# Moving one tile's normalise-and-Gelu step ahead of the other tile's statistics in a two-tile feed-forward block

## The reference

```python
x = _layernorm(x + attn(x))        # softmax over the query axis, causal mask
x = _layernorm(x + ffn(x))
def ffn(x):                        # three blocks
    h = x
    for blk in range(3):
        i0, i1 = (2 * blk, 2 * blk + 1)
        y = _qlora_linear(h, qweights[i0], ...)     # 1024 x 1024, dequantised, plus a rank-32 part
        y = _layernorm(y, ln_gamma[blk], ln_beta[blk])
        y = jax.nn.gelu(y, approximate=False)
        y = _qlora_linear(y, qweights[i1], ...)
        h = y + h
    return h
```

## Time and profile before

| | |
|---|---|
| median of 8 runs | 2744.24 us |
| the profiled execution | 2743.9 us |
| its span, slowest core (of 2724.1 to 2742.3) | 2742.3 us |
| TensorE busy with matmuls | 1659.6 us, 61% |
| VectorE busy | 1034.7 us, 38% |
| ScalarE busy | 1035.7 us, 38% |
| GpSimd busy | 130.3 us, 5% |
| mean granted clock of TensorE, slowest core | 0.795 |

### The profile page before, as it was taken

The page is one execution under the profiler, slowest core; times in us unless marked ns, Lnnn a source line. Parts: engine busy times, 40 slices in busy tenths (PEclk is TensorE's granted clock), DMA queues, the critical chain, the costliest instruction groups (busy, mean ns, idle before and its releaser), DMA issues.

```text
span 2742.3 us, 21892 instructions; the slowest of 8 cores (2724.1 to 2742.3 us)
## 1 busy us (share of the span) xinstructions
PE 1659.6 (61%) x6880; PEld 690.0 (25%) x6880; DVE 1034.7 (38%) x1001; ACT 1035.7 (38%) x1517; POOL 130.3 (5%) x112
## 2 busy tenths in 40 slices
PE   0999891396989111115658555776467656665853
PEld 0444330143433000002223222332123222222321
DVE  2113435301343734442532733255414526152262
ACT  0421113242111213324454445445454454545444
POOL 0000003300000500000000000000000000000000
PEclk9999995698999555557879758988678787687985
DMA  6200134501012086774100050110230000511001
GB/s 198 90 30 16 46 108 154 183 16 54 16 46 77 23 278 233 243 246 164 62 31 31 0 184 31 47 46 0 76 139 31 31 31 1 184 33 60 31 1 62
DMA packets 72542, 228.62 MB, mean 83 GB/s; under 512 B 6768, under 2 KB 7024, under 8 KB 66032
## 3 DMA queue, kind: packets, MB, share of 16 engines
q1 hardware_dynamic: 61680, 181.09, 20.0%
q0 software_dynamic: 10752, 46.14, 4.3%
HBM read 181.07 MB, written 46.14 MB: 83 GB/s over the span
## 4 chain that ended last, share of the span: by engine, by line
PE 48%; ACT 16%; DVE 13%; DMA 11%; issue 8%; PEld 2%; DVEq 1%; PEldq 1%; SPq 0%; ACTq 0%; POOL 0%; POOLq 0%
PE ps L857 23%; PE ps L298 8%; PE ps L420 5%; DMA weffs<-PL 4%; PE ps L361 4%; ACT PL L1033 3%; PE ps L837 2%; PEld ps L496 2%; PE ps L1085 2%; DVE PL L1025 2%; DVE PL L1023 2%; DMA PL<-xt 2%; DVE PL L627 2%; DVE PL L624 2%; PE ps L839 2%
## 5 line engine op out<-in xcount | busy, mean ns | idle before, releaser
L857 PE MATMUL ps<-PL 128*128 128x512 bf16 x3072 | 737.6, 397 | 249.2 <-ACT PL L1033 237.6
L857 PEld LDWEIGHTS ps<-PL 128*128 128x128 bf16 x3072 | 309.9, 101 | 655.7 <-issue 328.6
L298 PE MATMUL ps<-PL 128*128 128x512 bf16 x1024 | 229.9, 388 | 170.1 <-DVE PL L214 65.3
L1001 DVE TENSOR_TENSOR e2s<-e2s,m2s 128x512 f32<-128x512 f32 x32 | 22.1, 691 | 555.5 <-ACT e2s L993 555.5
L725 PE MATMUL ps<-PL 32*128 32x512 bf16 x48 | 28.1, 586 | 301.9 <-DVEq L748 205.3
L880 ACT ACTIVATE PL<-ps,fb 128x512 bf16<-128x512 f32 x192 | 131.9, 687 | 162.6 <-PE ps L839 162.3
L893 DVE SCALAR_TENSOR_TENSOR PL<-ps,fb,PL 128x512 f32<-128x512 f32 x192 | 144.2, 751 | 88.6 <-PE ps L857 88.1
L298 PEld LDWEIGHTS ps<-PL 128*128 128x128 bf16 x1024 | 101.6, 100 | 298.0 <-issue 183.2
L1085 PE MATMUL ps<-eye,PL 128*128 128x128 f32 x256 | 87.2, 436 | 142.8 <-ACT PL L1099 77.9
L496 PE MATMUL ps<-PL 128*128 128x512 bf16 x640 | 144.1, 390 | 20.2 <-ACTq L173 20.2
L420 PE MATMUL ps<-PL 128*128 128x512 bf16 x640 | 142.5, 385 | 7.8 <-issue 5.1
(11 more groups left out here) (80 smaller groups left out, 1725.9 us busy)
## 6 DMA issues: line engine op xcount, KB each, us to landing
PL<-weffs SPq DMA_DIRECT2D x24, 2048.0 KB, 9.4
PL<-xt SPq DMA_DIRECT2D x32, 1024.0 KB, 5.8
PL<-qw_t SPq DMA_DIRECT2D x48, 512.0 KB, 5.0
PL<-sc_t SPq DMA_DIRECT2D x48, 512.0 KB, 6.5
x1s<-PL POOLq DMA_DIRECT2D x16, 1024.0 KB, 10.3
PL<-x1s SPq DMA_DIRECT2D x64, 256.0 KB, 6.5
out<-PL POOLq DMA_DIRECT2D x32, 512.0 KB, 4.9
weffs<-PL POOLq DMA_DIRECT2D x48, 256.0 KB, 6.4
```

Of the source, the lines that this page charges most:

```text
L298: last = e.matmul(ps[bank][:], bfv(area + c * 512, 1024)[:, s * 128:(s + 1) * 128], xtbf[:, c * 2048 + tc * 512:c * 2048 + (tc + 1) * 512] ...
L857: last = e.matmul(ps[bank][:], bfv(WSL[sl], 8192)[:, c * 1024 + s * 128:c * 1024 + (s + 1) * 128], src_mv[:, c * 512:(c + 1) * 512], start ...
```

## The change

The even tile's `apply_gelu` is called right after the odd tile's first product and ahead of the odd tile's `ln_fin2`. The odd tile's `apply_gelu` is called where it was. The instructions are the same; their order changes on VectorE (even tile's L1023 and L1025 now ahead of the odd tile's L1001) and on ScalarE (even tile's L1033 now ahead of the odd tile's L992, L993, L1007 and L1009).

```diff
@@ -1141,9 +1141,12 @@
                 fin = {}
                 for t in ts:
                     y_mms(t, w1, wl[w1], cm[t], "y1", fbcols[w1])
+                    if t != ts[0]:
+                        gel[ts[0]] = apply_gelu(ts[0], blki, fin[ts[0]])
                     fin[t] = ln_fin2(t)
                 for t in ts:
-                    gel[t] = apply_gelu(t, blki, fin[t])
+                    if t not in gel:
+                        gel[t] = apply_gelu(t, blki, fin[t])
                 if w1 + 2 < 6:
                     if hook:
                         hook(w1 + 2)
```

## The result

The changed kernel takes 2693.37 us (median of 11 runs, 2690.49 to 2708.84) against 2744.58 us for the kernel before. The ratio is 0.9819, with a 95% interval of 0.98 to 0.9838: 1.8% faster, 51 us less by the medians. The ratio is of fast runs alone: some executions of each kernel ran longer, the cores of one die at a lower clock. The profiled execution has a span of 2694.3 us.

What follows compares the result with a forecast made beforehand. No engine is full, so work order sets the time, chiefly TensorE's 19.8 us wait per block for ScalarE's Gelu. Gains of 8 x 4.4 + 4 x 3.8 = 50.4 us from 2743.9 gave 2693.5 us, range 2672 to 2712.

Steps and rivals of the forecast that it cites:

- A's passes are hidden: VectorE: the even tile's passes, 8.95 us, fit its 26.97 us idle time at no cost; slowing of ScalarE's evacuations possible.
- A's second product starts 13.1 us sooner: TensorE: the even tile's second product starts 13.1 us sooner per block, the gross gain.
- The new stop at the fifth group, 5 to 7 us, ended by L893: TensorE, four banks full, waits 5 to 7 us per block for VectorE's first evacuation, held behind the odd tile's passes.
- The low clock at both stops, the first free, the second 2.25 us: TensorE restarts at 1.2 GHz after both idle times per block; the first is hidden, the second costs 2.25 us.
- 4.4 us per block: Net gain in each of 8 blocks: the last evacuation starts at 2191.3 instead of 2195.74.
- Third blocks bound by VectorE at 1.64 us per evacuation, gain 3.8: In each group's third block, VectorE's added addition makes 1.64 us per evacuation the limit; gain 3.8 us in four blocks.
- the lower bound, 2676: Clock not lowered at TensorE's second stop: 8 blocks gain 2.25 us more, the four VectorE-bound don't; 68 us, 2676.
- A table load more: Rival, ScalarE: splitting the neighbouring Gelus adds one table load of 1.28 us per block; 35 us gain, 2709; chance 0.06.
- No new stop: Rival: evacuations not held behind the odd tile's passes, its Gelus limit; gain 7.1 us per block, 2659; chance 0.05.
- nothing: Rival: an overlooked wait keeps the even tile's passes from starting sooner on VectorE; TensorE's wait stays 19.8 us, 2744; chance 0.04.
- slower: Rival: TensorE, stopped twice, stays at 1.2 GHz longer; with eight groups 7.2 us slower per block, 2830; chance 0.04.
- L1023 of A about 21 us ahead of B's subtraction: Profile sign on VectorE: the even tile's L1023 would start about 21 us ahead of the odd tile's subtraction.

Runs made afterwards that it cites:

- b_one_pass: Changed kernel with VectorE's multiplication by the reciprocal root left out for B, the odd tile; 2617.41 us, ratio 0.9535 to the kernel before.
- stats_mid: Changed kernel with the even tile's Gelus between the first half (square, copy) and second half (Ln, Exp) of the odd tile's statistics on ScalarE; 2682.9 us, ratio 0.9773.
- warm_after: Changed kernel with unneeded matmuls in TensorE's two stops, 28 ahead of the even tile's second product and 36 ahead of its fifth group; 2670.5 us, ratio 0.9733.
- vec_warm_all: vec_warm plus 20 unneeded matmuls in TensorE's 5.3 us stop in the odd tile's first product; 2621.38 us, ratio 0.9547.
- inter: vec_only with four of the even tile's eight Gelus between ScalarE's evacuations of groups 5 to 8 of the odd tile's first product; 2638.46 us, ratio 0.9607.
- vec_only: Kernel before with only VectorE's half of the change; ScalarE keeps its old order; 2671.8 us, ratio 0.973.
- inter_warm: inter plus unneeded matmuls at both places, 44 ahead of the even tile's second product and 20 in the odd tile's first; 2586.24 us, ratio 0.9418.
- vec_warm: vec_only plus 56 unneeded matmuls in TensorE's idle time ahead of the even tile's second product; 2643.86 us, ratio 0.9627.

## Why the prediction was right

It gave 2693.5 us; 2693.37 was measured. An agreement of 0.1 us is partly luck, since single terms are off by more. Point by point:

- *A's passes are hidden.* Right. They run at 2091.82 to 2100.76, and ScalarE's evacuations beside them keep their 0.69 us (L880: mean 687 ns before and after), so the pressure that I had left open isn't there.
- *A's second product starts 13.1 us sooner.* Right: 6.68 for 19.79 us of wait. This gross gain of 157 us is the 157 by which the wait on L1033 fell.
- *The new stop at the fifth group, 5 to 7 us, ended by L893.* Right, measured 5.4 to 7.1 us in the 24 blocks of cores 1 and 7, always after 32 matmuls. That the passes of B make it is shown by b_one_pass, and that it takes back what A's product gains is shown by stats_mid, where A's product starts 3.2 us later and nothing is lost.
- *The low clock at both stops, the first free, the second 2.25 us.* Right: in warm_after 2.2 per block behind the first evacuation, of which 1.9 arrive (22.9 us in all).
- *4.4 us per block.* Measured 4.5.
- *Third blocks bound by VectorE at 1.64 us per evacuation, gain 3.8.* The number is near (3.6) by luck, the mechanism wrong. Here is VectorE in a third block, two evacuations with work in hand:

```profile
2584.02 0.74 DVE L893 SCALAR_TENSOR_TENSOR PL<-ps,fb,PL 128x512 f32<-128x512 f32 x1
2584.87 0.69 DVE L903 TENSOR_TENSOR PL<-PL 128x512 f32<-128x512 f32 x1
2585.48 0.75 DVE L893 SCALAR_TENSOR_TENSOR PL<-ps,fb,PL 128x512 f32<-128x512 f32 x1
```

  An evacuation that waits for nothing follows the last by 1.46 us, not 1.64, because the next one starts before the one ahead has ended. VectorE caught up, and from restart to last evacuation third blocks take 22.9 to 23.8 us, as the others do (core 3). Much of their smaller gain was there before the change: on core 3 they took 72.9 us from A's subtraction to the last evacuation, the others 74.7, of which some 1.2 us lie between A's and B's subtraction (26.4 for 27.6). The trace says what makes that difference. In the kernel before, behind the 5.3 us stop in B's first product, the granted clock was 0.50 for 3.3 us on the mean in third blocks and for 4.9 in the others (all cores), and over the 96 blocks the stretch grows by 0.48 us per us of it. In vec_warm_all, with fillers in that stop, the stretch is 25.1 us in third blocks and 25.3 in the others. Why the low stretch is shorter in third blocks stays open.

  The same error stands in the lower bound, 2676. It lets third blocks gain nothing from a full clock; they do, in warm_after they take 22.1 us from first to last evacuation, for 24.2 in the changed kernel, and its 2670.5 us lie below that bound.
- *A table load more.* Out: L1033 has 24 loads, L992 24, L1007 32, in the kernel before as in the changed one. In `inter` too the numbers are the same. The Trainium skill, ScalarE: Activation LUTs, "Table sets: the hidden batching unit", says that cheap functions such as identity are in every table set; by the rows of `inter` the add and Square follow a Gelu without a load, so the set in use there has both. Of other sets they show nothing.
- *No new stop*, *nothing*, *slower*: none of them happened; in the block shown the clock was back at 1.00 some 4 us after the restart (0.83 in 2138 to 2140).
- *L1023 of A about 21 us ahead of B's subtraction.* Wrong, a slip that no term rests on: by the prediction's own times, 2124.3 and some 2155, it is 31, and measured are 29.3 (2091.82 to 2121.11). About 21 is VectorE's idle time in between, 20.35.

The step that nobody should copy is in my reading of the change as one thing. I worked out that B gains nothing and didn't draw the conclusion: if B's chain sets the end, moving A's Gelus ahead of it on ScalarE is the harmful half. vec_only shows it, 21.6 us.

## What to carry to other kernels

When a tile's work is moved ahead of its neighbour's on an in-order engine, work out both chains to the next shared resource. Here that was four PSUM banks: TensorE could run only four groups ahead of VectorE, and two thirds of the sooner start was lost there. Move a tile's work only on those engines that have idle time where it lands (VectorE did, ScalarE didn't), and look for gaps of one instruction's length before putting a block of eight in the way. An idle TensorE also pays afterwards: where the stops can't be removed, unneeded matmuls that end before the real ones can start were worth 22 to 28 us here in each of the three steps that added them by themselves, and 52 for two places at once (inter_warm against inter).

## What the hardware showed that I had not expected

**A third granted level.** In the changed kernel's profile cores 6 and 7 were granted 0.81 of the clock for 33 and 47 us in all, in two stretches each from about 2577 on; core 7, under dense matmuls:

```profile
2594.00:2598.00 4.00, 4.00 (x17) 1.65 (x16) 2.79 (x4) 1.08 (x1) 0.00 (x0) 0.81 0.00 0
2598.00:2602.00 4.00, 4.00 (x17) 1.63 (x15) 2.69 (x5) 1.36 (x3) 0.00 (x0) 0.81 0.00 0
```

Evacuations follow each other in 2.10 us there (2599.44 to 2601.54) in place of 1.73, and core 7's last block took 73.5 us against 69.5 on core 1. So the slowest core's span holds 4 us that are no part of the change. The Trainium skill, TensorE: Matmul & The Clock Gate, "Seeing it yourself", tells of a current limit of 13/16 of the clock for a whole die once three of its cores run dense matmuls. The level agrees (0.81); the reach doesn't: here two cores of the die show it and the other two don't, and the profiles of the kernel before and of the denser vec_warm, vec_warm_all and inter_warm have it on no core.

**The length of a stop doesn't tell alone whether the clock falls.** In stats_mid stops of 3.1 to 3.4 us were followed by products at full clock, while stops of 2.2 and 2.3 us weren't, nor those of 3.9 to 4.1 (core 3). Why is left open.
